# A four-layer transformer stack on one core: three layer-norm writes move to VectorE, the expert weights move into a later join, and one attention stage's side work takes other slots

## What is computed

```
x = ln(x + attn0(x)); x = ln(x + ffn0(x))   # 16 heads of 64; routed top-1, capacity, 8 experts
x = ln(x + attn1(x)); x = ln(x + ffn1(x))   # softmax(-distance), 16 heads of 8; routed top-2
x = ln(x + attn2(x)); x = ln(x + ffn2(x))   # grouped projections, 16 heads of 8; sign MLP
x = ln(x + attn3(x)); x = ln(x + ffn3(x))   # causal, 16 heads of 8; routed top-2 plus a shared MLP
_layernorm(x) = (x - mean) / sqrt(var + 1e-5)
```

```
mean_w = where(cnt > 0, w_tok.sum() / maximum(cnt, 1), 0)
out = out + mask[:, None] * eo * mean_w      # for each of 8 experts, 2 experts per token
```

## Time and profile before

| | |
|---|---|
| median of 3 executions | 2950.33 us (2945.1 to 2951.36) |
| profiled execution, its own time | 2950.33 us |
| its span | 2948.4 us |
| PE busy | 2350.3 us (80%) |
| ACT busy | 1478.3 us (50%) |
| DVE busy | 1449.3 us (49%) |
| POOL busy | 1331.5 us (45%) |
| moved by DMA | 153.43 MB |

### The profile page before, as it was taken

How to read it: one execution, slowest core, us unless ns; L and a number is a source line. 1 busy time by engine, 2 the same in 40 slices (tenths; PEclk the granted TensorE clock), 3 DMA queues, 4 the chain that set the end, 5 groups by cost and what they waited for, 6 DMA issues and landing times. The chain is left out here.

```text
span 2948.4 us, 52675 instructions
## 1 busy us (share of the span) xinstructions
PE 2350.3 (80%) x17978; PEld 1648.9 (56%) x17978; DVE 1449.3 (49%) x4042; ACT 1478.3 (50%) x3688; POOL 1331.5 (45%) x2068
## 2 busy tenths in 40 slices
PE   6999999994567999980599589996996999736850
PEld 4666666663554666650599345553553777524840
DVE  3555555553117999963233365672003666320743
ACT  4666666662336999970122156674222666512421
POOL 2444444443227888645533565531003454153255
PEclk9999999997776999995799698898997999967975
DMA  3000000002113222103111232220002322020212
GB/s 135 1 1 1 1 1 1 1 1 75 59 60 96 74 72 72 53 1 123 46 51 48 77 118 83 77 67 7 0 0 78 104 89 89 13 66 31 87 59 60
DMA packets 100389, 153.43 MB, mean 52 GB/s; under 512 B 16851, under 2 KB 69989, under 8 KB 93093
## 3 DMA queue, kind: packets, MB, share of 16 engines
q1 hardware_dynamic: 88356, 128.32, 13.7%
q0 software_dynamic: 11776, 21.81, 2.4%
HBM read 99.85 MB, written 48.24 MB: 50 GB/s over the span
## 5 line engine op out<-in xcount | busy, mean ns | idle before, releaser
L980 DVE TENSOR_REDUCE A_nmax<-A_S 128x2 f32<-128x512 f32 (+1 forms) x512 | 309.0, 620 | 220.8 <-PE A_S L766 110.9
L181 POOL TENSOR_SCALAR A_prob<-A_prob,A_rinv 128x256 f32<-128x256 f32 x512 | 235.4, 478 | 371.4 <-DVE A_rinv L433 371.4
L911 ACT ACTIVATE A_PT<-A_E 128x512 f32<-128x512 f32 (+1 forms) x512 | 275.2, 546 | 161.0 <-PE A_E L783 82.2
L428 DVE TENSOR_REDUCE A_nmax<-A_S 128x2 f32<-128x512 f32 x256 | 164.8, 685 | 161.0 <-PE A_S L271 161.0
L371 ACT ACTIVATE A_prob<-A_S,A_nmax 128x256 f32<-128x256 f32 x512 | 234.8, 477 | 4.9 <-DVE A_nmax L428 4.9
L1797 POOL COPY L_wr<-L_w 128x1024 f32 (+1 forms) x144 | 104.1, 724 | 240.8 <-PE L_k L1871 124.2
L1790 POOL DMA_INDIRECT sent<-x_state,row x160 | 154.6, 967 | 118.5 <-DVEq L2046 70.6
L1562 DVE TENSOR_SCALAR_CACHE_REDUCE A_D<-A_S 128x256 f32<-128x256 f32 x512 | 193.5, 417 | 15.8 <-PE A_S L1345 11.0
L1568 DVE COPY A_PT<-A_T 128x512 f32<-128x512 f32 x256 | 175.1, 686 | 20.1 <-PE A_T L1358 19.8
L1358 PE MATMUL A_T<-ident_sb,A_D 128*128 128x128 f32 x1024 | 161.1, 281 | 27.9 <-ACT A_D L1487 14.9
L1964 ACT ACTIVATE L_silus<-L_k 128x512 f32<-128x512 f32 x72 | 43.0, 597 | 261.3 <-PE L_k L1867 261.3
(11 more groups left out here) (382 smaller groups left out, 6030.8 us busy)
## 6 DMA issues: line engine op xcount, KB each, us to landing
A_QS<-stack_q SPq DMA_DIRECT2D x144, 192.0 KB
A_KS<-stack_k SPq DMA_DIRECT2D x144, 192.0 KB
L_xe<-sent SPq DMA_DIRECT2D x46, 256.0 KB
results<-L_ye SPq DMA_DIRECT2D x46, 256.0 KB
stack_q<-A_parts SPq DMA_DIRECT2D x48, 192.0 KB
stack_k<-A_parts SPq DMA_DIRECT2D x48, 192.0 KB
L_w<-f_w SPq DMA_DIRECT2D x24, 256.0 KB, 10.6
sent<-A_zeros SPq DMA_DIRECT2D x9, 512.0 KB
```

The lines of the kernel that those rows point to most:

```text
L181: nc.gpsimd.tensor_scalar(prob[:, n % NP, j, t, :], prob[:, n % NP, j, t, :], rinv[:, n % NP, j, t:t + 1], 1.0, ALU.mult, ALU.mult).then_i ...
L428: nc.vector.tensor_reduce(nmax[:, n % NP, j, :], psS[n % 2][j][:], AX.X, ALU.max, negate=True).then_inc(maxed, 1)
L911: nc.scalar.activation(PT[:, n % RING, :], psE[n % 2][:, 0:BLOCKS, :].rearrange("p a b -> p (a b)"), ACT.Exp, scale=scale).then_inc(expd, 1)
L980: nc.vector.tensor_reduce(nmax[:, b % 2, :, h], view, AX.X, ALU.max, negate=True).then_inc(maxed, 1)
```

## The change

1. In attn2 and attn3 the two writes of a normalised x (`write_last`, `write_x`) move from ACT to DVE, as `tensor_scalar` with subtract and multiply (x - mean, times rstd). The shift is no longer needed, so `root_last` and `root_var` have two POOL operations instead of four.
2. In attn1 `write_x` moves from POOL (slot 3) to DVE (slot 7, after `take_turned`).
3. The expert weight of ffn1 is not applied when the expert's output leaves PSUM; `take_y` becomes a plain copy. It is applied in `join_rows` of attn2: four `scalar_tensor_tensor` of 128x128 (row times its weight, plus sum) instead of two additions of 128x256. `mean_weights` now makes one weight per token and expert choice, with four operations on 128x32x8 instead of three on 128x72x8.
4. In `attention_small` the constants of the side work change. As slots modulo 16:

| step | engine | slot before | slot after |
|---|---|---|---|
| get_last (attn2) | POOL | 10 to 13 | 10 to 13, one batch later |
| join_rows (attn2) / join_acc (attn3) | DVE / POOL | 11 / 8 | 5 / 14 |
| stats_last | DVE | 12 | 6 (attn2), 3 (attn3) |
| root_last | POOL | 14 | 8 |
| write_last | ACT, then DVE | 2 | 10 |
| root_var | POOL | 3 | 2, behind the bias |
| write_x | ACT, then DVE | 8 | 7 |
| turn_new, take_new | PE, ACT | 10, 11 | 8, 9 |
| logits (attn3) | PE | 12 | 11 |

"One batch later" means that a batch's rows are fetched 54 slots ahead of its scores instead of 70.

The diff (left out at the dots: declarations, `root_last`, which changes as `root_var` does, and the body of attn1's `write_x` on DVE, which is that of attention_small):

```diff
--- before.py
+++ after.py
@@ -512,10 +512,10 @@
     NM_AT = 20
     OT_AT = LAG_O + 19
     ON_AT, Y_AT = OT_AT + 6, OT_AT + 9
-    F_AT, LG_AT = Y_AT + 11, Y_AT + 13
+    F_AT, LG_AT = Y_AT + 9, Y_AT + 12
-    GET_AT, NORM_AT = X_AT - 35, X_AT - 15
-    JOIN_AT, STATS_AT = (X_AT - 18, X_AT - 17) if last["K"] else (X_AT - 21, X_AT - 17)
+    GET_AT, NORM_AT = X_AT - 19, X_AT - 5
+    JOIN_AT, STATS_AT = (X_AT - 8, X_AT - 7) if last["K"] else (X_AT - 15, X_AT - 10)
     FIRST, LAST = GET_AT, SLOTS + Y_AT
...
@@ -567,7 +566,7 @@
         NMSTEPS = 4
-        JOINED = max(K, 1)
+        JOINED = TB * K if K else 1
@@ -668,12 +667,8 @@
                     pool.wait_ge(y_steps, 5 * (b + 1))
                     after(pool, x_done, TB * b)
                     nc.gpsimd.tensor_scalar(veps[:], mv[:, :, 1], EPS, None, ALU.add).then_inc(rooted, 1)
-                    pool.wait_ge(rooted, 4 * b + 1)
+                    pool.wait_ge(rooted, 2 * b + 1)
                     nc.gpsimd.tensor_tensor(rstd[:], veps[:], mhalf[:], ALU.pow).then_inc(rooted, 1)
-                    pool.wait_ge(rooted, 4 * b + 2)
-                    nc.gpsimd.tensor_tensor(shift[:], mv[:, :, 0], rstd[:], ALU.mult).then_inc(rooted, 1)
-                    pool.wait_ge(rooted, 4 * b + 3)
-                    nc.gpsimd.tensor_scalar(shift[:], shift[:], -1.0, None, ALU.mult).then_inc(rooted, 1)
...
@@ -712,14 +703,14 @@
                     if (b := at(s, QK_AT + 3)) is not None:
                         split_qk(b)
-                    if (b := at(s, Y_AT + 4)) is not None:
-                        root_var(b)
                     if (b := at(s, H + 1)) is not None:
                         split_max(b)
                     if (b := at(s, NM_AT + 1)) is not None:
                         send_max(b)
                     if (b := at(s, OT_AT - 4)) is not None:
                         add_out_bias(b)
+                    if (b := at(s, Y_AT + 3)) is not None:
+                        root_var(b)
@@ -926,26 +917,11 @@
-                def write_last(b):
-                    act.wait_ge(l_rooted, 4 * b + 4)
-                    for tile in range(TB):
-                        nc.scalar.activation(x_state[:, TB * b + tile, :], ly(b)[:, tile, :], ACT.Identity, bias=lshift[:, b % 2, tile:tile + 1],
-                                             scale=lrstd[:, b % 2, tile:tile + 1]).then_inc(x_ready, 1)
-
-                def write_x(b):
-                    act.wait_ge(rooted, 4 * b + 4)
-                    for t in range(TB):
-                        nc.scalar.activation(x_state[:, TB * b + t, :], y[:, t, :], ACT.Identity, bias=shift[:, t:t + 1], scale=rstd[:, t:t + 1]).then_inc(x_done, 1)
-
...
                 for s in range(FIRST, LAST + 4):
-                    if (b := at(s, NORM_AT + 4)) is not None:
-                        write_last(b)
-                    if (b := at(s, Y_AT + 9)) is not None:
-                        write_x(b)
                     if (b := at(s, F_AT + 1)) is not None:
                         take_new(b)
@@ -1006,12 +982,28 @@
...
+                def write_x(b):
+                    dve.wait_ge(rooted, 2 * b + 2)
+                    for t in range(TB):
+                        nc.vector.tensor_scalar(x_state[:, TB * b + t, :], y[:, t, :], mv[:, t, 0:1], rstd[:, t:t + 1],
+                                                ALU.subtract, ALU.mult).then_inc(x_done, 1)
+
                 def join_rows(b):
                     dve.wait_ge(fetched[b % 2], 16 * TB * K * (b // 2 + 1))
                     after(dve, x_ready, TB * (b - 1))
                     for k in range(K):
-                        after(dve, joined_x, K * b + k if k else 0)
-                        nc.vector.tensor_tensor(ly(b), lrows[:, b % 2, :, k, :], ly(b) if k else x_state[:, TB * b:TB * (b + 1), :], ALU.add).then_inc(joined_x, 1)
+                        after(dve, joined_x, JOINED * b + TB * k if k else 0)
+                        for tile in range(TB):
+                            nc.vector.scalar_tensor_tensor(out=ly(b)[:, tile, :], in0=lrows[:, b % 2, tile, k, :],
+                                                           scalar=last["weight"][:, k, TB * b + tile:TB * b + tile + 1],
+                                                           in1=ly(b)[:, tile, :] if k else x_state[:, TB * b + tile, :],
+                                                           op0=ALU.mult, op1=ALU.add).then_inc(joined_x, 1)
+
+                def write_last(b):
+                    dve.wait_ge(l_rooted, 2 * b + 2)
+                    for tile in range(TB):
+                        nc.vector.tensor_scalar(x_state[:, TB * b + tile, :], ly(b)[:, tile, :], lmv[:, b % 2, tile, 0:1], lrstd[:, b % 2, tile:tile + 1],
+                                                ALU.subtract, ALU.mult).then_inc(x_ready, 1)
                 def stats_last(b):
                     dve.wait_ge(joined_x, JOINED * (b + 1))
@@ -1031,6 +1023,8 @@
                         join_rows(b)
                     if (b := at(s, STATS_AT)) is not None:
                         stats_last(b)
+                    if (b := at(s, NORM_AT + 2)) is not None:
+                        write_last(b)
                     if (n := head(s)) is not None:
                         row_max(n)
                     if causal and (b := at(s, H)) is not None:
@@ -1039,7 +1033,9 @@
                         normalise(b)
                     if (b := at(s, Y_AT + 2)) is not None:
                         norm_stats(b)
-                    if onward["gate"] is not None and (b := at(s, LG_AT)) is not None:
+                    if (b := at(s, Y_AT + 8)) is not None:
+                        write_x(b)
+                    if onward["gate"] is not None and (b := at(s, LG_AT + 1)) is not None:
                         take_logits(b)
 
@@ -1235,12 +1231,6 @@
                     pool.wait_ge(rooted_var, 2 * b + 1)
                     nc.gpsimd.tensor_tensor(rstd[:], veps[:], mhalf[:], ALU.pow).then_inc(rooted_var, 1)
-                def write_x(b):
-                    pool.wait_ge(rooted_var, 2 * b + 2)
-                    for t in range(TB):
-                        nc.gpsimd.tensor_scalar(x_state[:, TB * b + t, :], y[:, t, :], mv[:, t, 0:1], rstd[:, t:t + 1],
-                                                ALU.subtract, ALU.mult).then_inc(x_done, 1)
-
...
@@ -1590,6 +1579,12 @@
...
+                def write_x(b):
+                    dve.wait_ge(rooted_var, 2 * b + 2)
...
@@ -1618,6 +1613,8 @@
                         normalise(b)
                     if (b := at(s, Y_AT + 2)) is not None:
                         norm_stats(b)
+                    if (b := at(s, Y_AT + 7)) is not None:
+                        write_x(b)
...
@@ -2093,10 +2089,9 @@
                     link(nc.vector.tensor_scalar(cnt[:], cnt[:], 1.0, None, ALU.max))
                     link(nc.vector.reciprocal(mean[:], cnt[:]))
                     link(nc.vector.tensor_tensor(mean[:], mean[:], wsum[:], ALU.mult))
-                    link(nc.vector.tensor_tensor(past[:], numbers[:, 0:E].unsqueeze(1).to_broadcast([P, Q, E]),
-                                                 tile_of[:].unsqueeze(2).to_broadcast([P, Q, E]), ALU.is_equal))
-                    link(nc.vector.tensor_tensor(past[:], past[:], mean[:].unsqueeze(1).to_broadcast([P, Q, E]), ALU.mult))
-                    nc.vector.tensor_reduce(tile_mean[:], past[:], AX.X, ALU.add).then_inc(meant, 1)
+                    for k, sel in enumerate((sel1, sel2)):
+                        link(nc.vector.tensor_tensor(d[:], sel[:], over_t(mean), ALU.mult))
+                        link(nc.vector.tensor_reduce(weight[:, k, :], d[:], AX.X, ALU.add))
...
@@ -2158,10 +2153,6 @@
...
-                    elif mean2:
-                        dve.wait_ge(meant, 1)
-                        i = nc.vector.tensor_tensor(ye[:, q % 2, :, :], by_tile(psY[q % 2]),
-                                                    tile_mean[:, QUAD * q:QUAD * (q + 1)].unsqueeze(2).to_broadcast([P, QUAD, P]), ALU.mult)
                     else:
                         i = nc.vector.tensor_copy(ye[:, q % 2, :, :], by_tile(psY[q % 2]))
                     i.then_inc(y_out, 1)
```

11 lines of the change are left out of this document (4 added, 7 removed).

## The result

The changed kernel takes 2983.08 us (median of 4 runs, 2979.73 to 2988.38); the kernel before, with one more run beside it, 2947.72 us (4 runs, 2944.34 to 2951.36). The ratio is 1.0121 (95% interval 1.0100 to 1.0143): 35 us slower. The profiled execution of the changed kernel took 2990.81 us (span 2989.0), that of before 2950.33 (span 2948.4), so the two traces differ by 40.5 us.

The account below looks back on a forecast made before the run. Bounds: ACT in attn1 with DVE close behind, PE in attn3, no full engine in attn2, where PE's waits lengthen batches. Terms 6 - 0.9 - 3.4 + 5.4 + 3.5 + 0 - 0.4 - 0.4 - 0.3 = +9.5 on 2950.3 gave 2960 us, range 2940 to 2982.

Parts of the forecast that it names:

- The sign: Whole kernel: the change makes it slower, given a chance of 0.58.
- the likeliest case: Whole kernel: the forecast itself, terms summing to +9.5 us, 2960 us (2952 to 2970), chance 0.45.
- rival C: attn1's idle room absorbs the write pair and attn2's gather delay does not count: 2950.3 us, no change; chance 0.22.
- attn1, write_x: Steady attn1: two writes on DVE cost 1.4 us per batch, less 0.95 room, over 12 batches: +6 us.
- Rival B: attn1: DVE becomes the bound, each write held for a whole POOL operation, +25 us, 2979 us; chance 0.13.
- attn1, end: Last batch of attn1: two uncovered POOL operations become 0.62 us on DVE, -0.9 us.
- ffn1: ffn1: a plain copy out of PSUM saves little, mostly behind PE; taken as 0.
- attn2, start: Start of attn2: four gathers instead of eight precede the first root, so the first score comes earlier, -3.4 us.
- attn2, gathers one batch later: attn2: gathers lie beside one more batch's scores, lengthening two batches by 3.1 and 2.3 us: +5.4 us.
- attn2, gathers behind root_last: attn2: gathers start 0.5 us later behind root_last, delaying PE's results in seven batches: +3.5 us.
- moves within the batch: attn2: join leaving slot 11, write_last ahead of slot 10's maximum and the longer join in slot 5: 0 in all.
- attn3: Steady attn3: PE busy 182.00 of 182 us covers everything, so 0.

Follow-up runs that it names:

- e10: Changed kernel with the gathers of attn2 one batch earlier, on chip 15: 2971.7 us, 1.0049 of the kernel before.
- e14: Changed kernel with attn2's gathers one batch earlier, ffn1's scaling and the plain two-addition join (in slot 5), chip 13: 2960.9 us, 1.0070 of the kernel before.
- e13: Changed kernel with ffn1's scaling and the join's two plain additions as before, join still in slot 5, chip 13: 2976.1 us, 1.0101 of the kernel before.
- e16: Changed kernel with attn2's four gathers per batch replaced by plain SP loads from fixed rows (other numbers computed), chip 13: 2934.2 us, 0.9974 of the kernel before.
- e17: Changed kernel with attn2's gathers in slots 1 to 4, on chip 9: 2935.4 us, 0.9930 of the kernel before.
- e18: Kernel before with its attn2 gathers in slots 1 to 4, on chip 9: 2993.0 us, 1.0129 of the kernel before.
- e1: Changed kernel with all slots of attention_small as before, on chip 2: 2966.6 us, 1.0297 of the kernel before.
- e3: Changed kernel with gathers set to slots 13 to 16, which left every engine's instruction order the same, chip 2: 2883.4 us, 1.0010 of the kernel before.
- e5: Kernel before, unchanged, traced on chip 7, where the kernel before measured 2878.9 and 2880.2 us.
- e6: Changed kernel, unchanged, on chip 7: 2882.6 us, 1.0012 of the kernel before.

## Why the prediction was wrong

The sign was right, the size not: 2983 lies just above the range, and the likeliest case gave +9.5 where the traces show +40. The step that failed is the price of the late releases in attn2, put at +3.5 and 0. The sign is in part luck: on the two chips without late releases the change costs 2.4 to 3.4 us, which is rival C.

- **attn1, write_x**: forecast +6, found about half: batches 4 to 14 together take 270.0 to 270.2 us with the write on POOL and 273.2 to 273.4 with it on DVE, in every trace, and the whole stage, its end included, takes 2.6 us more on the average (the +0.6 of the table is the smallest such difference). The price of a pair came out right, 1.34 us against 1.4, but by luck: I took one operation as held and the other as free, and both are held. I also misread the row from attn0. POOL's first operation there runs from 106.03 for 0.48, and the DVE operation of 0.510 ends at 106.59, 0.08 us behind it, as in attn1. So it too was held to the end of POOL's, and my sum of a wait and the whole own length (0.75) was the wrong measure. By the Trainium skill ("SBUF — State Buffer", "Who interferes with whom") the engine that comes second to the shared ports is blocked fully while the other's instruction lasts. The trace agrees on the full block (0.08 us behind POOL's end in 24 of 32 writes); it does not show the order so plainly, since the write of 1142.27 was recorded 0.06 us ahead of POOL's cast and was held all the same. What failed in the sum is the subtraction: DVE's waits shrank to 2.4 us, ACT, busy 287 of 290 us, went on setting the pace, and a steady batch grew by 0.1 us and not 0.5. Rival B had the mechanism and the wrong consequence.
- **attn1, end; ffn1; attn2, start**: -0.9, 0, -3.4 forecast. Found -2.4 at the end (3.1 late at the last copy, 0.7 at the last turn_new), -0.8, -1.7. Small, and together right: -4.9 for -4.3.
- **attn2, gathers one batch later**: +5.4 forecast, 19 measured (e10) and 15 (e14 against e13). The two batches I named did what I said (24.8 and 19.7 for 23.2 and 20.1). The rest is in the others, which are no longer alike; why, no run shows.
- **attn2, gathers behind root_last, and moves within the batch**: +3.5 and 0 forecast; this is the term that failed, some +12 to +20 (e10 and e14 against before). I had read from the earlier trace rows that there are late releases and that they go with the gathers. But I priced the shift by the 0.5 us that POOL is later. What counts is what the other engines have left to do while nothing is released: before, DVE had normalise and the join there, and the stall showed as pieces of 1.57 and 0.64 us:

```profile
1876.31 0.69 DVE L980 TENSOR_REDUCE A_nmax<-A_S 128x2 f32<-128x512 f32 x1 [1.57 <-PE A_S L769]
1879.41 0.69 DVE L980 TENSOR_REDUCE A_nmax<-A_S 128x2 f32<-128x512 f32 x1 [0.64 <-DMA A_KS<-stack_k]
```

The second of these is 3.63 us late, and DVE was idle for 0.64 of it. After, DVE and ACT have run dry, and the stall stands in full, 2.2 to 3.3 us per batch, with the lower clock behind it. Over the stage DVE has 12 late results in both kernels, with 6.0 and 20.6 us of idle time. Shown are these stalls, that they are absent without POOL's indirect DMAs (e16) and with the gathers in other slots (e17, e18), and that the loss goes with them. How the 40 us divide between the idle time and the clock behind it is argued, not measured.
- **attn3**: 0 forecast, 0 found (first score to last turn_new 317.0 and 316.8 us).
- **ffn3**: +5.6 in the pair of traces, not in the forecast. Its length varies between 378 and 387 us from trace to trace on these chips, and no part of the change touches its code. On chip 15 the changed slots have 385 and 387, the slots of before 380 and 381; on chip 13 the changed kernel has 379. Whether these 5 us belong to the change stays open.
- That the whole loss hangs on the chip, +0.1% on two chips and +1.2 to +1.4% in three other measurements, was in no rival. Nothing in the trace of before could tell that its "remote" waits are not there on other chips.

## What to carry to other kernels

Don't price an instruction that is moved by its own length, but by what else stands in that slot: the same write took 0.34 us free and 0.74 beside POOL's work, and a few such operations in unlucky slots cost 86 us on a chip where the changed kernel lost 3 (e1 and e3). An operation that is held ends just behind the one that holds it, so price it by what is left of that one. Where PE's results come late while POOL issues gathers, don't put four of them in a row where PE waits for DVE; spread them between other work of POOL (shown on one chip, e17), and leave the join enough time behind the last of them: 7 us were too few in e18, and with 16 us, in the changed kernel's steady batches, it did not wait. Look for idle time that an order of work happens to cover before moving that work away. And measure on more than one chip before a change of 1% is called a loss or a gain.

## What was not expected of the hardware

- Two kinds of chip: the same program takes 2880 us on two and 2941 to 2957 on three. In the two traces of before the difference is all in two pieces in which POOL issues indirect DMAs close together while PE works (attn2 33 us, ffn3 41 us), as waits for "remote" that the other chips don't have. attn1, with gathers 5.9 us apart, has none.
- A DVE write or join operation that POOL's work holds up ends 0.08 us behind POOL's operation (`tensor_scalar`, all 24 held writes of attn1) or 0.14 to 0.15 us behind it (the join), even where it was recorded up to 0.06 us ahead: 1.93 us next to one of 1.89, 1.20 instead of 0.35 beside POOL's split.
- Two stops of PE per batch, with 2.48 and 2.62 us from scores to scores, went with a granted clock of 0.72 in attn2; with 1.26 and 2.42 us (e5) or 1.26 and 1.58 (e6) it was 1.00.
